# Storing the second table's blanks and the later weights from SyncE, one table for the first two groups of edges, and two groups scored ahead of the mix branch

## The reference, cut to what matters

```
xn = layernorm(x)
# graph attention (edges src -> dst)
xl = xn @ W_l ; xr = xn @ W_r
e = xl[src] + xr[dst] ; e = max(e, 0.2 e)
score[edge, head] = sum over the head's 64 channels of e * att
softmax of the scores over each dst, weighted sum of xl[src]
# mix branch
h = layernorm(xn) * g + b ; xm = h @ Wx + bx
q, k, v from xm (softmaxes), kv = k^T v, attn = (q kv) @ Wo
fx = attn + xn ; mlp(layernorm(fx)) with gelu, W1 (256x1024), W2 (1024x256)
x = x + gnn(xn) + mix(xn)
```

## Time and profile before

| | |
|---|---|
| median of 3 runs | 1285.03 us (1281.55 to 1287.8) |
| profiled execution, first to last instruction | 1281.2 us, PE clock granted 0.876 on average |
| its time beyond that span | not recorded; the runs shown lie 0.4 to 6.6 us above the span |
| busy: PE / DVE / ACT / POOL | 75% / 60% / 37% / 37% |
| start of the kernel to the first scatter | 78.8 us |
| early and late groups (turns 2 to 31) | 77 to 549 us |
| softmax and sum of layer 0, experts, layer 1 | 550 to 1281 us |

### The profile page before, as it was taken

One profiled execution on the slowest core, in us unless ns is written; L12 is line 12 of the kernel. 1 busy time (PEld: TensorE's weight loads), 2 busy tenths in 40 slices (PEclk: granted clock), 3 DMA queues, 4 the chain that ended last, 5 costly groups with the idle time before them and its releaser, 6 DMA issues.

```text
span 1281.2 us, 19622 instructions
## 1 busy us (share of the span) xinstructions
PE 962.1 (75%) x6816; PEld 835.0 (65%) x6816; DVE 771.1 (60%) x1800; ACT 468.7 (37%) x786; POOL 471.1 (37%) x371
## 2 busy tenths in 40 slices
PE   4387999688888878737625999926891992899992
PEld 1356887587778867627625899924691782788881
DVE  6368479767867676888675444324889657333322
ACT  2045756557765767135411111101460250111110
POOL 1448788878878787610002222130000000211103
PEclk9697999899999999877757999967896995899996
DMA  8942232222222222178005899850000002577662
GB/s 285 281 123 63 62 67 73 65 53 61 55 61 65 59 57 41 17 190 201 1 20 185 301 306 312 302 197 24 1 1 0 1 1 70 216 257 259 234 229 70
DMA packets 57996, 155.86 MB, mean 122 GB/s; under 512 B 23341, under 2 KB 33506, under 8 KB 49674
## 3 DMA queue, kind: packets, MB, share of 16 engines
q1 hardware_dynamic: 25500, 116.31, 27.6%
q0 software_dynamic: 25056, 24.10, 8.4%
q10 hardware_dynamic: 7378, 14.67, 3.5%
HBM read 133.82 MB, written 20.89 MB: 121 GB/s over the span
## 4 chain that ended last, share of the span: by engine, by line
PE 42%; DVE 19%; DMA 12%; issue 12%; POOL 10%; ACTq 2%; ACT 2%; POOLq 0%; DVEq 0%; SPq 0%
PE bank L697 13%; PE bank L708 6%; DMA pair_scores<-sc_ring,idx_ring 6%; POOL pair_scores L1745 4%; POOL arena L1735 4%; PE bank L645 4%; DMA arena<-row_tab,ids 4%; PE bank L481 3%; PE bank L443 3%; PE bank L433 3%; PE bank L459 2%; PE bank L634 2%; ACTq L1543 2%; POOL arena L1800 2%; PE bank L762 1%
## 5 line engine op out<-in xcount | busy, mean ns | idle before, releaser
L1790 POOL DMA_INDIRECT arena<-row_tab,ids x42 | 58.7, 1398 | 573.3 <-DVE ids L1312 505.5
L1745 POOL DMA_INDIRECT pair_scores<-sc_ring,idx_ring x160 | 215.9, 1349 | 70.4 <-issue 50.7
L697 PE MATMUL bank<-arena 128*128 128x128 f32 (+1 forms) x1616 | 198.3, 280 | 0.0
L1735 POOL DMA_INDIRECT arena<-xl_tab,idx_ring x120 | 163.4, 1362 | 93.3 <-issue 32.6
L697 PEld LDWEIGHTS bank<-arena 128*128 128x128 f32 (+1 forms) x1616 | 186.3, 189 | 7.7 <-issue 3.6
L1324 DVE TENSOR_TENSOR arena<-bank,arena 128x512 f32<-128x512 f32 (+2 forms) x76 | 37.2, 509 | 150.5 <-ACT arena L1628 150.5
L708 PE MATMUL bank<-arena 128*128 128x256 f32 (+1 forms) x404 | 99.0, 388 | 0.0
L459 PE MATMUL bank<-tab 125*128 125x314 bf16 x400 | 66.8, 321 | 32.5 <-DVE tab L916 32.5
L1515 ACT ACTIVATE late_ohT<-arena 125x875 fp32r<-125x875 f32 x100 | 90.7, 927 | 0.0
L1628 ACT ACTIVATE arena<-bank 128x512 f32<-128x512 f32 (+2 forms) x76 | 32.4, 450 | 147.7 <-PE bank L697 147.7
L481 PE MATMUL bank<-late_hi,late_ohT 125*125 125x256 f32 x500 | 84.1, 299 | 0.6 <-DVE arena L882 0.6
(11 more groups left out here) (308 smaller groups left out, 1929.3 us busy)
## 6 DMA issues: line engine op xcount, KB each, us to landing
arena<-in_exp SPq DMA_DIRECT2D x25, 1024.0 KB, 5.4
arena<-in_exp SPq DMA_DIRECT2D x17, 1364.0 KB
arena<-in_exp0o SPq DMA_DIRECT2D x25, 512.0 KB, 5.3
arena<-pair_scores SPq DMA_DIRECT2D x10, 1093.8 KB
arena<-in_exp1o SPq DMA_DIRECT2D x17, 640.0 KB
pair_scores<-cnt SPq DMA_DIRECT2D x5, 1093.8 KB
pair_scores<-cnt ACTq DMA_DIRECT2D x5, 1093.8 KB
slot_y<-arena ACTq DMA_DIRECT2D x42, 128.0 KB, 4.9
```

Source lines behind the costliest of these rows:

```text
L697: mm = pe.matmul(banks[1 + 2 * q + buf][0:rows, i * SLOTS:(i + 1) * SLOTS], w_in(s, q, k, m, rows), xsT[:, s, k, :], start=(k == 0), stop= ...
L1735: p.indirect_dma_start(out=gat[:, b % 2, 0, j * D:(j + 1) * D], out_offset=None, in_=xl_tab, in_offset=bass.IndirectOffsetOnAxis(ap=idx_ri ...
L1745: p.indirect_dma_start(out=pair_scores[which], in_=sc_ring[:, b % 2, j, :], in_offset=None, out_offset=bass.IndirectOffsetOnAxis(ap=idx_ri ...
L1790: p.indirect_dma_start(out=xs[:, s, :], out_offset=None, in_=tab, in_offset=bass.IndirectOffsetOnAxis(ap=ids[:, s, :], axis=0))\
```

## The change

- `node_neg`, the bias of the one-hot rows, is computed by DVE before it waits for `x`, not after the `lr` copies.
- SP stores 3 of table 0's 5 blanks first, then the vectors, biases and `wx`/`wo` weights, then `xl_tab` tile by tile as each tile of `lr` is read out (10 transfers and not 2), then the other 2 blanks, `mixw`/`mixk`, the rows of groups 2 and 3, and only then the 10 blanks of table 1 and the later vectors and weights, all from SP. ACT issues no transfer any more.
- `SINGLE` goes from 0 to 2: groups 0 and 1 scatter into table 0 alone, so each of their 10 scatters waits for the one before it, and POOL waits for table 1's blanks only ahead of `turn(4)`.
- DVE scores group 0 before its half of `mixhT`, and group 1 where group 0 was; PE makes group 1's rows ahead of `xm`; ACT makes group 1's one-hots right after group 0's. Every later group moves one place up in the three lists, and the addition of `bo` moves from before `mixhT` to after `xm`.

```diff
-SINGLE = 0
+SINGLE = 2
@@ PE
-            pe.wait_ge(sem("w0_in"), 16)
             pe.wait_ge(sem("mixh"), 1)
             to_fm("mixhT", ta)
+            early_rows(1, 0, 1, 2)
+            pe.wait_ge(sem("w0_in"), 16)
             read_out(pe, "mixhT")
             linear_fm("xm", fb_, "wx", K2)
...
-            early_rows(1, 0)
+            early_rows(2, 0)
...
-            early_rows(10, 0, 1, 2)
             count_group(5, 1)
             early_rows(11, 0, 1, 2)
@@ DVE
             v.memset(mixk[:, :, :], 0.0).then_inc(sem("mixw0"), 1)
+            dve.wait_ge(sem("iotas"), 5)
+            v.tensor_scalar(node_neg[:, :], node_f[:, :], -1.0, None, ALU.mult).then_inc(sem("node_neg"), 1)
             dve.wait_ge(sem("x_in"), 16 * len(PARTS))
...
             affine(ta, 0, "ln1_g", "ln1_b", sem("mixh"))
-            own.note(v.tensor_tensor(tb[:, :, :], xn[:, :, :], V(0, "bo"), ALU.add))
+            score_early(0)
             from_fm("mixhT", fb_)
...
-            score_early(0)
+            own.note(v.tensor_tensor(tb[:, :, :], xn[:, :, :], V(0, "bo"), ALU.add))
+            score_early(1)
...
-            score_early(10)
             onehots(6, 0)
+            score_early(11)
             onehots(7, 1)
-            score_early(11)
             onehots(8, 0)
@@ ACT
             hot_rows(0, 0, 0)
-            act.wait_ge(sem("tables"), 16 * len(PARTS))
-            (10 blanks of table 1, vec0b, w0b, w2 issued from ACT)
+            hot_rows(1, 1, 0)
             from_fm("mixhT", fb_)
             act.wait_ge(sem("fb_in"), 16)
             biased("xm", fc, FB_BX)
-            hot_rows(1, 1, 0)
+            hot_rows(2, 0, 0)
@@ POOL
-            pool.wait_ge(sem("tables"), 16 * len(PARTS))
+            pool.wait_ge(sem("tables"), T * 16 * len(PARTS))
@@ SP
-            blank_first()
-            read_out(sp, "lr")
-            for rows in PARTS:
-                sp.dma_start(xl_tab.rearrange("(t p) d -> p t d", p=P)[rows], xlr[rows, :, 0:D])\
-                    .then_inc(sem("tables"), 16)
+            blank(0, range(3))
             (vec0, fb, wx/wo weights)
+            for t in range(T):
+                read_out(sp, "lr", t)
+                for rows in PARTS:
+                    sp.dma_start(xl_tab[t * P:(t + 1) * P, :][rows], xlr[rows, t, 0:D]).then_inc(sem("tables"), 16)
+            blank(0, range(3, T))
             (mixw, mixk)
             for g in range(2, 4):
                 edge_rows(g, g % 2, 0)
+            blank(1, range(T))
+            (vec0b, w0b, w2 issued from SP)
             for g in range(4, LATE):
                 edge_rows(g, g % 2, 0)
```

More of the change, by code:

```diff
@@ L569, in _ @@
             hidden_mix(0, 1)
-            early_rows(4, 1, 2)
+            early_rows(5, 1, 2)
             hidden_mix(2, 3, 4)
-            early_rows(5, 0)
+            early_rows(6, 0)
             hidden_mix(5, 6, 7)
-            early_rows(5, 1, 2)
+            early_rows(6, 1, 2)
             read_out(pe, "m1")
@@ L578, in _ @@
             output_mix(0, 1)
-            early_rows(6, 0)
+            early_rows(7, 0)
             output_mix(2)
-            early_rows(6, 1, 2)
+            early_rows(7, 1, 2)
             output_mix(3, 4)
-            early_rows(7, 0, 1, 2)
+            early_rows(8, 0, 1, 2)
             read_out(pe, "m2")
@@ L1045, in _ @@
             v.tensor_tensor(q4, q4, spread(qsu), ALU.mult).then_inc(sem("qsoft"), 1)
-            add_rows(1, 0)
+            add_rows(2, 0)
             bank, freed = got(dve, "kN")
@@ L1053, in _ @@
                 v.tensor_copy(fd[0:32, 1, off:off + w], bank[0:32, 0:w]).then_inc(freed, 1)
-            add_rows(1, 1, 2)
-            score_rows(1)
+            add_rows(2, 1, 2)
+            score_rows(2)
             bank, freed = got(dve, "kv")
@@ L1059, in _ @@
                 .then_inc(freed, 1)
-            add_rows(2, 0)
+            add_rows(3, 0)
             for c, (off, w, _) in enumerate(CHUNKS):
@@ L1064, in _ @@
                 v.tensor_copy(fb_[:, 1, off:off + w], bank[:, 0:w]).then_inc(freed, 1)
-            add_rows(2, 1, 2)
-            score_rows(2)
+            add_rows(3, 1, 2)
+            score_rows(3)
             for t in range(T):
@@ L1086, in _ @@
             add_mix(0, 1)
-            add_rows(6, 0)
+            add_rows(7, 0)
             add_mix(2)
-            add_rows(6, 1, 2)
-            score_rows(6)
+            add_rows(7, 1, 2)
+            score_rows(7)
             add_mix(3, 4)
@@ L1539, in _ @@
             hot_rows(0, 0, 0)
-            act.wait_ge(sem("tables"), 16 * len(PARTS))
-            for m in range(T):
-                for rows in PARTS:
[L1543 to L1549, removed]
+            hot_rows(1, 1, 0)
             from_fm("mixhT", fb_)
@@ L1562, in _ @@
                 a.activation(fb_[:, 0, off:off + w], bank[:, 0:w], ACT.Copy).then_inc(freed, 1)
-            hot_rows(3, 1, 0)
             hot_rows(4, 0, 0)
+            hot_rows(5, 1, 0)
             from_fm("h2T", fb_)
             biased("m1", mlp, FB_B1, ACT.Gelu, range(0, 2))
-            hot_rows(5, 1, 0)
+            hot_rows(6, 0, 0)
             biased("m1", mlp, FB_B1, ACT.Gelu, range(2, 8))
-            for g in range(6, 10):
+            for g in range(7, 11):
                 hot_rows(g, g % 2, 0)
             read_counts(0)
-            hot_rows(10, 0, 0)
             split_counts(0)
@@ L1819, in _, with blank @@
                 sp.dma_start(dsti[rows], dst_in[rows]).then_inc(sem("edges_in"), 16)
-            def blank_first():
-                for m in range(T):
+            def blank(w, tiles):
+                for m in tiles:
                     for rows in PARTS:
-                        sp.dma_start(cells[0][m][rows], cnt[rows, :, :].rearrange("p m n -> p (m n)")[:, 0:H * NC])\
-                            .then_inc(sem("blank0"), 16)
+                        sp.dma_start(cells[w][m][rows], cnt[rows, :, :].rearrange("p m n -> p (m n)")[:, 0:H * NC])\
+                            .then_inc(sem(f"blank{w}"), 16)
             def edge_rows(g, s, late):
@@ L1856, in _ @@
                 edge_rows(g, g % 2, 0)
+            blank(1, range(T))
+            sp.dma_start(vec[:, V_FIRST:V_SIZE0], vec0_in[V_FIRST:].partition_broadcast(128))\
+                .then_inc(sem("vec0b_in"), 16)
+            sp.dma_start(wres[:, :, n_w1:W_SIZES[0]], w0_in[:, :, n_w1:]).then_inc(sem("w0b_in"), 16)
+            sp.dma_start(w2, w2_in).then_inc(sem("w2_in"), 16)
             for g in range(4, LATE):
```

30 lines of the change are left out of this document (14 added, 16 removed).

## The result

The changed kernel takes 1291.22 us in the median of 5 runs (1288.57 to 1293.09); beside it the kernel before took 1284.3 us (1280.65 to 1287.8, 5 runs). The ratio is 1.0067, with a 95% interval of 1.0042 to 1.0093: slower by about 9 us. (The ratio weighs all rounds; the two medians alone differ by 6.9 us.) The forecast was 1266 us and a range of 1254 to 1277.

The account below looks back on a forecast made before the run. It took POOL's turns, with PE close behind, as the pace after a start held up by ACT's transfers. `turn(4)` 19 us earlier, carried to the end, gave 1285 - 19 = 1266 us, range 1254 to 1277.

Parts of the forecast that it names:

- The hole at 50 us: From 50 to 60 us PE, DVE and ACT do nothing, while the DMA engines are 94% busy.
- R3: Rival: group 0's gathers land late, at 47 to 50; `turn(4)` at 100, 10 us gained, 1275 us (1272 to 1278); chance 0.16.
- the price of a scatter in `turn(2)`: Serial scatters into one table beside blanks and weights: 6 us each, 27 us in all, `turn(2)` ends at 76.
- 4.5 us of a scatter under load: Estimate from the skill's 2 us HBM access at high load: `turn(2)` ends near 70, total some 6 us lower.
- a quiet chain costs nothing: Scatters start 3.05 us apart and a quiet one lands in 2.7 us, so alone the single-table chain costs nothing.
- its term: `turn(3)` takes 15.3 us, as before the change, from 76 to 91.5.
- The prediction's own sign of this: Sign that the prediction is wrong: the last scatter moves less than `turn(12)`.
- a lead is carried to 549 us: POOL and PE that start earlier carry their lead to 549 us; from there everything hangs on the last scatter.
- PE goes along: Up to the late groups PE gains 18.5 us: `xm` 11 us earlier and one group (about 7.5 us) less.
- The forecast's 19 us: `turn(4)` starts at 92 (84 to 100) instead of 110.84, and the whole kernel gains those 19 us.
- The rival that ended slower: R5, the single table: past 6.2 us per scatter in both turns `turn(4)` comes later; at 8 us 1303 us; chance 0.04.

Follow-up runs that it names:

- the mended seam: Changed kernel with `onehots(7, 1)` back ahead of `score_early(11)`: 1281.44 us, ratio 1.0009; the same with two tables from the start: 1273.41 us, 0.9949.
- the run with the blanks held: Changed kernel with SP's store of table 1's blanks and later weights held until all ten scatters of groups 0 and 1 landed: 1295.05 us, one run.
- the two kernels at 0.995: Changed kernel with two tables from the start: one with `onehots(7, 1)` ahead of `score_early(11)`, 0.9949; one with old PE and DVE lists from group 1 on, 0.9945.

## Why the prediction was wrong

**The parts, by the runs.** One table for groups 0 and 1 costs 0.67% in the kernel before, 0.69% in the changed one (1.0067 over 0.9998) and 0.60% beside the mended seam (1.0009 over 0.9949). The seam costs 0.58% with one table (1.0067 over 1.0009), 0.49% with two, and 0.29% in the kernel before. What is left, ACT free of transfers, SP's order, and group 0 scored early, gains 0.5% (0.9949, 0.9945). Multiplied, 0.9949 x 1.0060 x 1.0049 is 1.0058, which the interval of the change holds. Each quotient has an uncertainty of about 0.35%, estimated from the intervals of its two ratios: the signs agree everywhere, the sizes are rough.

**Right.** The first gather at 28.6 (forecast 31, bounds 30 and 34, so earlier than either), group 0 scored at 47.9 (49), `xm` done at 54.2 (57.5), group 1 scored at 65.5 (66), no issue on ACT at the start, and no wait of ACT that mattered. The hole at 50 us was what the profile said it was, and closing it moved `xm` by 15 us. Two slips in the sums decided nothing: 8.9 MB at the rate of the earlier trace rows are 24 us and not 27 (SP issued them from 41.70 to 68.66), and R3's `turn(2)`, from 55, would by its own 27 us end at 82 and not 85.

**Wrong: the price of a scatter in `turn(2)`.** The forecast chose 6 us, "since only one is in flight", between 3.05 and 8. The four intervals were 15.0, 9.6, 6.3 and 3.4 us, 34.3 in all for 24. The upper bound of 8 us was no bound. It was worked out from the earlier trace rows for the 125 packets of one DMA, but "only one is in flight" was not so either. DVE's timeline, the start of group 1's scores:

```profile
59.16 1.62 DVE L883 TENSOR_TENSOR arena<-arena,bank 125x512 f32<-125x512 f32 x3 [3.07 <-DMA arena<-xl_tab,idx_ring]
```

DVE waits until 59.16 for gathers of group 1, the last of which POOL had issued by 45.8. So the first scatter, issued at 50.25, stood in its queue behind gathers of group 1 and the first one of `turn(2)`. The queue moved 462 packets from 50 to 66 us, 29 a us, more than the 16 a us of the earlier trace rows and half the 56 a us of the earlier trace rows; its share of the engines' time was 9.1%, against 18.0% there. How much of the 15.0 us is the gathers ahead of the scatter and how much its own, no run shows. That the load is the cause, the run with the blanks held shows: there DVE does not wait for group 1's gathers, and the scatters are 3.4 to 4.1 us apart. The Trainium skill, page "DMA: Bandwidth & Descriptors", section "Latency and other measured facts", by which the prediction made 4.5 us of a scatter under load, is further off still: the trace has 15.0 and 9.6 us for the first two.

**Wrong: a quiet chain costs nothing.** The 2.7 us of the last scatter, from its start to SP's next issue, was carried over to a chain on POOL, and there scatters start 3.4 to 4.1 us apart even with no store beside them. Whether the gather behind each scatter or POOL's own wait makes the difference, no run shows. So `turn(3)` took 18.7 us and not 15.3. Both errors together put `turn(4)` at 104.75 and not at 92: `turn(2)` took 37.3 us for 27, `turn(3)` 3.4 us more than its term. Group 2 was scored at 94.0 and not at 84, since its gathers sit in the same turn as the slow scatters.

**Wrong: an edit left without a price.** The diff of DVE's list shows `onehots(7, 1)` moved behind `score_early(11)`. The forecast looked at the start alone and took "from `turn(4)` on both kernels use two tables and the same lists". They are not the same lists there. This edit costs 6 to 7 us, nearly as much as the 8 to 9 of the single table, and without it the change is not measurably slower than the kernel before (1.0009, 0.9982 to 1.0036). The prediction's own sign of this came true: `turn(12)` was 3.6 us earlier, and the last scatter 5.9 us later.

**Half right: a lead is carried to 549 us.** With two tables and a mended seam, a lead of 6.4 us at `turn(4)` is 7.6 us when group 12 is scored, and the time falls by 6.5 us. In the profiles the last scatter comes 9.5 us earlier (539.66 for 549.15) and the span is 5.8 us shorter, so some of the lead is lost behind the last scatter, where the experts of layer 0 take about 3.5 us longer. So POOL's lead counts, as the forecast said. But it is POOL's alone. "PE goes along" was no part of the gain: in the two kernels at 0.995 the mix branch and group 1 stand in opposite order, and neither is measurably faster; PE, early, only has less to do from 110 to 242 us. And the part of POOL's lead that one can have is small: with two tables POOL must wait for the blanks until 71, and with one it waits for its own scatters. Either way `turn(4)` comes at 103 to 107. The forecast's 19 us needed both waits to be cheap.

**The rival that ended slower** named the right mechanism, the single table, but had it decide only past 6.2 us for each scatter, held in both turns. The mean from 48.7 to 104.75 was 5.6 us, below that point, so `turn(4)` came earlier than before, and with the single table but without the seam the time is that of the kernel before (1.0009). The sign came from the two together, and the forecast had priced one by its load alone and the other not at all.

**What stays open.** The part of the 9 us that lies in the experts of layer 0 in the profiles (3.4 us), and whether SP's new order causes it; why POOL's instructions in turns 4 to 11 add up to 2 us more with the single table; how the 15.0 us of the first scatter divide; and whether the seam really costs the kernel before only half as much (its interval, 0.03% to 0.56%, holds the 0.49% and nearly reaches the 0.58%).

**A better version.** The change with `SINGLE = 0` and `onehots(7, 1)` back ahead of `score_early(11)` takes 0.9949 of the time before (0.9927 to 0.9971), and 1.2% less than the change as made (0.9949 over 1.0067).

## What to carry to other kernels

A chain of small transfers in which each waits for the one before it must be priced by the time of one landing under the load that lies beside it, with all that is still ahead of it in its own queue, and a queue's rate with many in flight does not give that. When a wait is removed by making something else serial, work out both waits to the first point where they meet again (here the start of `turn(4)`): that difference is the gain, not the earlier start. And in a list written by hand every line that changes place is an edit with a price, the ones at the far end of the diff too: ask of each which engine waits for it and what now stands ahead of it.

## What the runs showed of the hardware

- In a chain in which each waits for the one before, an indirect scatter of 125 rows took 15.0, 9.6, 6.3 and 3.4 us to the next one's start, beside stores on another queue that held 89.0%, 87.6%, 57.7% and 14.1% of the 16 engines' time; ahead of the first, gathers were still in its own queue. With no blanks or weights beside it the chain took 3.4 to 4.1 us (3.4 to 5.2 in the kernel before with one table), and the last scatter of the kernel before landed in 2.7 us.
- From 50 to 66 us the two queues did not share evenly: 89.0% and 9.1% of the 16 engines' time, the bulk queue in packets of 8.1 KB in the mean (4.30 MB in 531). With the bulk queue silent the indirect one, still a chain, used 16.5%.
- Issuing the same 10 blanks took SP 20.43 us beside POOL's indirect DMAs and 18.71 us without them late in the kernel; ACT took 21.61 us and SP at the start 16.62 us. In the other kernels with SP's new order it took 16.3 to 21.7 us, so that POOL's DMAs make it slower is not shown.
